# Fewer and moved idle products on TensorE, and another spread of the quantising work, in a twelve-stage perceiver kernel

## The reference

```python
x = x + sublayer(layernorm(x), ...)
```

```python
s  = max(max(|block|) / 7, 1e-12)
wq = clip(round(block / s), -8, 7) * s
```

## Time and profile before

| | |
|---|---|
| time of the kernel before, median of 3 runs | 1540.85 us (1539.77 to 1543.25) |
| the profiled execution's own time | 1540.85 us |
| its span, first to last instruction | 1539.0 us |
| PE busy | 1442.0 us (94%) |
| DVE busy | 930.2 us (60%) |
| ACT busy | 764.8 us (50%) |
| mean granted clock of PE | 0.983 of full speed |

### The profile page before, as it was taken

How to read it: one execution, slowest core, us unless ns; L and a number is a source line. 1 busy time by engine, 2 the same in 40 slices (tenths; PEclk the granted TensorE clock), 3 DMA queues, 4 the chain that set the end, 5 groups by cost and what they waited for, 6 DMA issues and landing times. The chain is left out here.

```text
span 1539.0 us, 29773 instructions
## 1 busy us (share of the span) xinstructions
PE 1442.0 (94%) x11414; PEld 1093.6 (71%) x11414; DVE 930.2 (60%) x2890; ACT 764.8 (50%) x1793; POOL 80.8 (5%) x78
## 2 busy tenths in 40 slices
PE   7997999998899889999999999999999798889987
PEld 6887989975677554577767777777766696666765
DVE  4754556557667342577777777777777276444434
ACT  5854545433122131476667666666776691323222
POOL 2210000000000000200000000000000000000000
PEclk9998999998999899999999999999999999999999
DMA  8956535411247299311111111001100300507760
GB/s 280 352 180 226 146 95 165 123 42 66 106 177 274 79 326 367 154 38 37 37 38 37 38 37 37 11 28 38 37 2 2 127 1 1 234 1 276 265 252 4
DMA packets 82812, 182.30 MB, mean 118 GB/s; under 512 B 5872, under 2 KB 58608, under 8 KB 81264
## 3 DMA queue, kind: packets, MB, share of 16 engines
q1 hardware_dynamic: 81952, 171.98, 31.8%
q10 hardware_dynamic: 720, 8.42, 1.3%
HBM read 179.86 MB, written 0.52 MB: 117 GB/s over the span
## 5 line engine op out<-in xcount | busy, mean ns | idle before, releaser
L2061 ACT ACTIVATE cross_s<-cross_s,cross_shift 128x896 f32<-128x896 f32 x224 | 215.1, 1031 | 35.1 <-DVE cross_shift L2145 35.1
L2055 ACT COPY cross_eT<-cross_ring 128x512 f32<-128x512 f32 x280 | 153.1, 591 | 143.4 <-PE cross_ring L1983 143.4
L1983 PEld LDWEIGHTS cross_ring<-consts,cross_s 128*128 128x128 f32 x1568 | 169.9, 142 | 56.1 <-issue 43.4
L1983 PE MATMUL cross_ring<-consts,cross_s 128*128 128x128 f32 x1568 | 198.5, 279 | 6.3 <-ACT cross_s L2061 6.3
L2136 DVE CUSTOM_DVE_ANT_0 cross_s<-cross_scores,cross_mask,cross_top 128x448 f32<-128x448 f32 x224 | 141.3, 681 | 83.2 <-PE cross_scores L1972 83.1
L493 ACT ACTIVATE slots_probs<-slots_scores,slots_bias,ctx_rinv 128x128 f32<-128x128 f32 x294 | 130.2, 458 | 106.8 <-DVE slots_bias L535 106.8
L155 PE MATMUL slots_scores<-slots_qkT,slots_ctxT 128*128 128x128 f32 x1176 | 142.5, 281 | 9.3 <-DMA slots_ctxT<-in_ctxT 8.7
L2136 DVE CUSTOM_DVE_ANT_0 cross_s<-cross_scores,cross_mask,cross_half_max 128x448 f32<-128x448 f32 x224 | 141.2, 680 | 15.3 <-PE cross_scores L1972 15.3
L155 PEld LDWEIGHTS slots_scores<-slots_qkT,slots_ctxT 128*128 128x128 f32 x1176 | 141.2, 197 | 13.0 <-DMA slots_ctxT<-in_ctxT 9.9
L388 PE MATMUL slots_attended<-ctx_rows,slots_probs 128*128 128x257 f32 x588 | 134.2, 380 | 1.7 <-DVE slots_pooled L549 1.0
L388 PEld LDWEIGHTS slots_attended<-ctx_rows,slots_probs 128*128 128x128 f32 x588 | 108.6, 190 | 16.9 <-issue 1.5
(11 more groups left out here) (809 smaller groups left out, 2108.2 us busy)
## 6 DMA issues: line engine op xcount, KB each, us to landing
ctx_rows<-in_ctx_rows SPq DMA_DIRECT2D x28, 896.0 KB, 8.0
ctx_rows<-in_moe_w SPq DMA_DIRECT2D x24, 1024.0 KB, 10.2
slots_ctxT<-in_ctxT SPq DMA_DIRECT2D x42, 512.0 KB, 4.1
slots_ctxT<-in_ctxT SPq DMA_DIRECT2D x42, 384.0 KB, 4.7
cross_ctxT<-in_ctxT SPq DMA_DIRECT2D x13, 896.0 KB, 4.7
padded_ctxT<-in_ctxT SPq DMA_DIRECT2D x12, 896.0 KB, 4.6
plain_ctxT<-in_ctxT SPq DMA_DIRECT2D x12, 896.0 KB, 4.7
local_layers<-in_w_local SPq DMA_DIRECT2D x2, 4552.0 KB, 14.5
```

The source lines that it names most:

```text
L1983: last = pe.transpose(bank(("turn", u, t))[:, j * P:(j + 1) * P], s_buf[:, u % 2, j, t * P:(t + 1) * P], K.ident)
L2055: act.copy(eT[:, u % 2, t], bank(item)).then_inc(st("emptied_act"), 1)
L2061: act.activation(rows, rows, ACT.Exp, bias=shift[:, u % 2, j:j + 1], scale=SCALE).then_inc(st("exp"), 1)
```

## The change

The change does two things. It gives the 28 quantising pieces another split over nine places instead of ten: the place ahead of `block_keys` is dropped, the place ahead of the row maxima is moved behind them, each following place moves with it (between copies and outputs, behind the outputs), and the place between the two maxima of `f` is dropped. And it removes idle products at eleven places, lowers their number at two, raises it at five, and adds them at two new places; over the execution they become 19 fewer.

```diff
-Q_SPLIT = (1, 1, 1, 7, 2, 2, 2, 2, 4, 6)
+Q_SPLIT = (2, 4, 4, 2, 2, 3, 4, 5, 2)
...
# stage_pattention, PE
                 attend16(pe, K, st, "sdpa", heads, headsT, pr, prT, v, o_mm)
-                idle_products(pe, K, p_idle, 1)
                 pe.wait_ge(st("o"), 1)
...
                 turn("p", "p_exp")
-                idle_products(pe, K, mm, 1)
                 pe.wait_ge(st("p_probsT"), 1)
...
# stage_pattention, DVE
                 inverse("v")
-                rest.some(dve, Q_SPLIT[0])
                 K.weights.wait(dve, "patt")
...
+                maxima_vector(dve, st, "sdpa", heads, small[:, 0, :], 4)
+                rest.some(dve, Q_SPLIT[0])
+                copies_vector(dve, st, "sdpa", prT, headsT, 4)
                 rest.some(dve, Q_SPLIT[1])
-                maxima_vector(dve, st, "sdpa", heads, small[:, 0, :], 4)
-                copies_vector(dve, st, "sdpa", prT, headsT, 4)
+                outputs16(dve, link, st, o, o_mm, small[:, 1, :])
                 rest.some(dve, Q_SPLIT[2])
-                outputs16(dve, link, st, o, o_mm, small[:, 1, :])
                 dve.wait_ge(st("oT_mm"), 1)
                 dve.tensor_scalar(oT[:, :], oT_mm, D ** -0.5, None, ALU.mult).then_inc(st("oT"), 1)
                 rest.some(dve, Q_SPLIT[3])
...
                     link(dve.tensor_reduce(top["f"][:, j:j + 1], f_sc[:, j * 512:(j + 1) * 512], X_AXIS, ALU.max, negate=True))
-                    if j == 0:
-                        rest.some(dve, Q_SPLIT[7])
                 dve.tensor_tensor(top["f"][:, 2:3], top["f"][:, 0:1], top["f"][:, 1:2], ALU.min).then_inc(st("f_top"), 1)
                 link(dve.tensor_tensor(K.x, K.x, x2[:, :], ALU.add))
-                rest.some(dve, Q_SPLIT[8])
+                rest.some(dve, Q_SPLIT[7])
...
                 dve.tensor_copy(efT[:, 4:8], fT_mm[:, 4:8]).then_inc(st("f_probsT"), 1)
-                rest.some(dve, Q_SPLIT[9])
+                rest.some(dve, Q_SPLIT[8])
...
# stage_quantised, between the transposes of o and the wait for oT
-                idle_products(pe, K, tr, 2)
...
# stage_folded_attention: ahead of ln_done; ahead of q; ahead of v
-                idle_products(pe, K, sc, 2)
+                idle_products(pe, K, sc, 4)
-                idle_products(pe, K, sc, 16)
+                idle_products(pe, K, sc, 14)
-                idle_products(pe, K, mm, 4)
...
# stage_experts, ahead of ln_done
-                idle_products(pe, K, wide, 4)
+                idle_products(pe, K, wide, 5)
...
# stage_cross_heads, ahead of the first transposes
-                    if u == 0 and tiles[0] == 0:
-                        ring.await_free(pe, ("turn", 0, 0))
-                        idle_products(pe, K, bank(("turn", 0, 0)), 5)
                     pe.wait_ge(st("exp"), SETS * (u + 1))
...
# stage_delta: ahead of ln_done
-                idle_products(pe, K, b[6], 3)
+                idle_products(pe, K, b[6], 4)
# ahead of EI of the last level; of inv_rows; of u
-                    if n == LEVELS - 1:
-                        idle_products(pe, K, b[0], 1)
-                idle_products(pe, K, b[0], 1)
-                idle_products(pe, K, b[0], 1)
# ahead of stats (new); ahead of o
+                idle_products(pe, K, b[6], 5)
-                idle_products(pe, K, b[7], 10)
+                idle_products(pe, K, b[7], 15)
...
# stage_local, each of the two layers: behind the scores; between the two
# turn_groups; ahead of o; ahead of n2
-                    idle_products(pe, K, big[2], 6)
+                    idle_products(pe, K, big[2], 3)
-                    idle_products(pe, K, big[2], 2)
-                    idle_products(pe, K, big[2], 1)
-                    idle_products(pe, K, big[2], 5)
+                    idle_products(pe, K, big[2], 6)
...
# stage_mqa: behind the two mask products, ahead of ln_done; ahead of qkv
+                idle_products(pe, K, mm2, 2)
-                idle_products(pe, K, mm, 7)
```

## The result

The changed kernel takes 1555.98 us (median, 1551.15 to 1558.33), the kernel before 1539.77 us beside it: a ratio of 1.0105, 95% interval 1.0086 to 1.0125, so 16.2 us or 1.05% slower. The forecast was 1554.0 us. The profiled execution of the changed kernel took 1554.31 us, 13.5 us over that of before. Its page: busy time of PE, and the granted clock in 40 slices.

A forecast was written before the change was run, and what follows sets the result against it. It took PE's waits between dense stages and falls of its granted clock as what counts. Clock terms 7.4, added products 4.05 and pieces 1.65 us sum to 13.1 us on 1540.85: 1554.0 us, range 1544.5 to 1560.

The forecast's parts named there:

- Local stage, 4.6 us: Local stage, two layers: removed idle products let the clock fall in each, 2.3 us a layer; bounds 0 and 8.
- The pieces, 1.65 us: Quantising pieces: delays of 1.8, 0.55, 0.25 and 0.75 us, less 1.7 gained at the end, net 1.65 us slower.
- The tail of the pieces, 1.7 us gained: Behind the last product, two pieces replace six, so the residual waits less for DVE: 1.7 us gained.
- Multi-query, 0.9 and 0.85 us: Multi-query stage: 0.9 us for half clock behind the removed run, 0.85 us for two idle products added behind the masks.
- Folded, 0.6 and 0.5 us: Folded stage: 0.6 us for the clock after removals ahead of `v`, 0.5 us for products added ahead of the layernorm.
- Cross, 0.5 us: Cross stage: a 2.6 us gap from removed products slows the transposes behind it, 0.5 us; bounds 0 and 1.9.
- Delta, 0.8, 0.6 and 1.3 us: Delta stage: 0.8 us for the clock after removals, 0.6 and 1.3 us for products added ahead of `stats` and `o`.
- Experts, 0.4 us: Experts stage: two more records at the end of the idle run delay the transposes by 0.4 us.
- Quantised, 0: Quantised stage: what is left around the removed products is either dense or at half clock already, so 0.
- Rival 1: Thin work holds the clock; local, folded, cross and delta terms fall away, 6.5 us, giving 1547.5 us; chance 0.22.
- Rival 2: Added products hold the clock and the kernel gets faster, 1534.8 us with all 10 us gained; chance 0.10.
- Rival 3: The same gains, from 1 to 7 us, cancel the delays: 1538 to 1544, about 1541 us; chance 0.07.

The follow-up runs named there:

- the local stage put back: The changed kernel with the local stage's idle products back at their earlier numbers, except ahead of the second layernorm's transposes: 1547.79 us, 1.0069 of the kernel before.
- both causes undone: The changed kernel with the local stage's idle products put back and the first quantising pieces ahead of the row maxima: 1540.75 us, 1.0018 of the kernel before.
- the pieces moved: The kernel before with only the new quantising split, its first two pieces ahead of the row maxima: 1538.61 us, 1.0002 of the kernel before.
- the fastest version: The kernel before plus idle products at waits, with more in the slots, experts and cross stages: 1530.76 us, 0.9948 of the kernel before.

## Why the prediction was right, and where it wasn't

The direction and the size were right (13.1 us forecast, 16.2 measured). Two terms were too small, by 4.6 us (local) and 6.3 us (pieces). That the total is as near as 3.1 us is in part luck: the measured parts sum to 21.0 us (17.7 by the medians), and stages moved by 1.5 us and more with falls that also come and go without the change.

- **Removed products give back 0, and falls follow in the thinned stretches.** Shown. A run with the local ones gone and one with thin ones in their place are both slower by 8 to 9 us. The local stage takes 82.80 to 83.17 us and has no fall in the ten profiles with its products in place, and 86.56 to 91.52 us with a fall in seven of eight layers in the four without. The other removals show as well. In the four profiles that have them (the changed kernel, the removals alone, the local stage put back, both causes undone) a fall follows the removed products of the folded, delta and multi-query stages in all four, those of the cross stage in three and those of the quantised stage in two; in the ten other profiles none stands at these places.
- **Local stage, 4.6 us.** Undersized: 7.1 us in the profile after (6.7 without the 0.4 of the products added there), 7.6 to 8.7 where products were only removed. The step that fell short is "I take 2.3 a layer": it let a fall catch the transposes of o and `wo`. In layer 0 it caught `wo` alone (1.7 us); in layer 1 it caught the products with v too and went on over the idle run ahead of `n2` (5.4 us, above the 4 a layer that the prediction allows).
- **The pieces, 1.65 us.** The mechanism was right for the first 1.8 us, "with them PE's products of group 0 and everything behind". The sum took them as a delay alone and did not ask what a PE that stands still for 2.03 us does to the clock of the transposes behind, which it had asked everywhere else. Measured: 8.0 us alone (7.2 by the medians), 0.3 with the pieces moved. The stage takes 47.98 to 50.21 us in the eleven profiles with the copies on time and 52.40 to 53.39 us in the three with late ones. It has falls in all fourteen, 6.8 to 10.2 us long in sum in the eleven and 13.6 to 17.1 in the three. So the late copies don't bring a fall that wasn't there; they go with longer ones, which catch the transposes and products of the attention. That this is what they cost beyond their delay is read from these profiles, not tested by itself. The medians differ by more than the profiled stages do. In part that is the choice of the profile: the one of the pieces alone is the fastest of its nine executions (1540.66 us), with a mean granted clock of 0.984, where the middle one of the nine has 0.980. The rest stays open.
- **The tail of the pieces, 1.7 us gained.** It came: counted from the stage's start, the last product begins 4.8 us later than before (at 49.35 us for 44.53), but the residual only 3.2 us (51.39 for 48.15), for it now waits 0.35 us for PE and no more for DVE's pieces. What was too small are the delays ahead of it, 3.35 us in the sum and 4.8 here.
- **Multi-query, 0.9 and 0.85 us.** The fall behind the gap came as forecast (2.05 to 3.65 us), the added products alone made the stage 1.02 us longer. Yet the stage is only 0.43 us over before, since the start was not cold in this execution, worth 1.5 us. Against the 24.26 us of unchanged stages with no cold start it is 1.93 us longer, for 1.75 forecast.
- **Folded, 0.6 and 0.5 us.** The stage is 1.04 us longer, with the removals alone 1.12 us. The added products cost next to nothing where the start was at full clock (37.00 us with them, 36.87 without).
- **Cross, 0.5 us.** The 16 records take 3.41 us behind a wait of 2.51 (before 1.99). The stage is 600.64 us with this fall and one over its last 0.5 us. It is 599.22 us in the fastest version, which has no fall there but more idle products, and 600.12 in the run of the delta stage's additions, whose one fall covers the last 1.9 us: so the fall behind the gap costs 0.5 to 1.4 us. It didn't show in the difference, because the falls at 616.4 and 1203.5 of the kernel before were absent.
- **Delta, 0.8, 0.6 and 1.3 us.** The profile shows 5.2 us, of which up to 2.5 also came without any change to the stage; 2.7 remain, and 2.7 were forecast. The removals alone left the stage at 89.88, so their 0.8 is not seen. Of the 1.3 ahead of `o` the rows show 2.8: 9.29 us of idle records for 6.50.
- **Experts, 0.4 us.** The transposes start 2.23 us behind the idle run's start instead of 1.80, 0.4 us late as worked out; but the stage is no longer (55.90), and 55.5 to 56.2 in all profiles. The delay is absorbed further on, where PE waits for weights: 1.60 us for DMA at 603.76 in the kernel before, 1.14 us at the same product in the changed one.
- **Local n2, 0.4 us.** 83.17 us for the stage in the three profiles that have the added products and no fall there, 82.80 to 82.83 without them: 0.37 us.
- **Quantised, 0.** This zero is in doubt. The 12 records behind the two removed products take 4.54 us for 2.86, in a fall from 409.6, and the stage is 35.92 us where it is 34.23 with no fall. With both causes undone it is 35.92 us again, with a fall at the same place; with the local products back it is absent (34.23 us). None of the ten profiles with the two products in place has it. So "either dense or at half clock already" missed up to 1.7 us, in some executions.

Together: the removals outside the local stage, 2.8 us in the sum, are not seen in the whole times (9.1 for all, 9.2 for the local ones, each to some 3 us), the additions came to 3.9 for 4.05 (2.0 by the medians), and the two undersized terms made up for more than that.

**The rivals.** Rival 1, that thin work holds the clock, is out: it gave 82.8 us for the local stage, which took 89.86. The gap of 3.6 us brought a fall, as the Trainium skill (TensorE: Matmul & The Clock Gate, "Why this matters for your kernels") warns of idle gaps; but falls also came with no gap over 1.52 us, and even with PE busy for 3.50 of 4.00 us, so its warning, read as being of gaps alone, covers too little. Rival 2, that the added products hold the clock, is out as to this change: alone they are 3.9 us slower. Rival 3, where gains cancel the delays, is out with it, as the whole is 16.2 us slower. The mechanism of the two may be at work even here, where the delays outweigh it: the mean granted clock of the twelve executions with the additions alone is 0.985, of the kernel before beside them 0.983. At other places it pays: products added to waits, not ahead of ready work, gave 5.7 to 8.0 us.

## What to carry to other kernels

Here an idle product at a wait that ended later anyway cost nothing, and taking it out saved nothing; judge it by the stretch of real work behind it, which doubles if the clock falls. Here full products of 256 columns held the clock and products of 4 columns in their place did not, though PE looked equally busy; put them into waits rather than ahead of work that is ready. When work is moved on a helper engine, ask not only by how much it delays PE, but how thin PE gets meanwhile: two pieces of 0.9 us between a reduction and the copies that PE waits for cost 7 to 8 us, and nothing that can be seen one place earlier.

## What the runs showed of the hardware

- Products of 4 columns kept PE's records busy (3.50 of 4.00 us ahead of a fall) and the run was as slow as with nothing in their place: 1.0050 [1.0026, 1.0073] against 1.0060 [1.0036, 1.0083]. In the fastest version a fall came behind 4.00 us with 3.78 us of records, most of them of 17 columns.
- The falls of one kernel differ from execution to execution: the folded stage took 39.05 and 36.87 us, slots 324.06 and 318.79 us. The place and the length of a fall set its price: 1.7 us for 3.4 us of half clock in one layer, 5.4 for 13.7 in the other, with the same instructions.
